# Experts' results finished in their tile of places and scattered to the output, instead of stored and gathered back

## The reference, cut to what matters

```python
xt = layernorm(x2)                         # 1250 x 512
probs = softmax(xt @ Ws + bs)              # 8 experts
prob_max, routes = max(probs), argmax(probs)
y = gelu(xt @ W1[e] + b1[e]) @ W2[e] + b2[e]     # for the token's e = routes
out = x2 + y * prob_max
```

## Time and profile before

| | |
|---|---|
| median of 3 runs | 1897.75 us (1884.08 to 1905.15) |
| the profiled execution | 1896.57 us, of which its span is 1894.8 us |
| busy: TensorE, VectorE, ScalarE, GpSimd | 83%, 68%, 47%, 58% |
| mean granted TensorE clock | 0.922 of full speed |
| from the first gather of the expert loop (1795.18 us) to the end of the span | 99.6 us |
| from the last bias add of the loop (ends 1871.46 us) to the end of the span | 23.3 us |

### The profile page before, as it was taken

The page is one execution under the profiler, slowest core; times in us unless marked ns, Lnnn a source line. Parts: engine busy times, 40 slices in busy tenths (PEclk is TensorE's granted clock), DMA queues, the critical chain, the costliest instruction groups (busy, mean ns, idle before and its releaser), DMA issues.

```text
span 1894.8 us, 20582 instructions
## 1 busy us (share of the span) xinstructions
PE 1570.2 (83%) x6464; PEld 672.8 (36%) x6464; DVE 1282.0 (68%) x2339; ACT 882.9 (47%) x977; POOL 1103.7 (58%) x1073
## 2 busy tenths in 40 slices
PE   2767877877798888987899988987999989888594
PEld 1223333332343333332433333333433333333573
DVE  6678876778246898777437867875458868765333
ACT  1454434445215556665316656664056666741120
POOL 4777777776016667776036777772067777740022
PEclk8898989888899999999899999998999999999597
DMA  6677666676147767776257787763388887755344
GB/s 221 199 200 200 178 194 186 181 233 203 48 116 225 204 199 211 208 208 181 64 164 229 229 245 225 227 196 106 96 245 231 236 247 221 210 147 191 113 131 154
DMA packets 119349, 355.34 MB, mean 188 GB/s; under 512 B 19760, under 2 KB 24200, under 8 KB 118981
## 3 DMA queue, kind: packets, MB, share of 16 engines
q0 software_dynamic: 83600, 274.01, 50.8%
q1 hardware_dynamic: 35637, 79.95, 13.1%
HBM read 333.93 MB, written 19.95 MB: 187 GB/s over the span
## 4 chain that ended last, share of the span: by engine, by line
PE 45%; POOL 16%; DVE 12%; DMA 10%; issue 8%; ACT 8%; DVEq 0%; SPq 0%; POOLq 0%; ACTq 0%
PE ps L1467 42%; POOL ring L683 14%; DVE ring L856 7%; ACT ring L1315 6%; DMA zT<-slot_table 6%; DMA ring<-x_table,idxT 3%; PE ps L1532 2%; DVE aggT L1166 1%; DVE xT L1066 1%; POOL ring L726 1%; DMA mix<-in_edge_weight 0%; ACT zT L1414 0%; DVE lg L900 0%; PE ps L1845 0%; POOL ring L735 0%
## 5 line engine op out<-in xcount | busy, mean ns | idle before, releaser
L683 POOL DMA_INDIRECT ring<-x_table,idxT x1018 | 1058.7, 1040 | 590.4 <-issue 294.7
L856 DVE SCALAR_TENSOR_TENSOR ring<-we_bc,wT,ring 128x512 f32<-128x512 f32 x1018 | 689.9, 746 | 126.5 <-DMA ring<-x_table,idxT 126.3
L1315 ACT ACTIVATE ring<-ring 128x3072 f32<-128x3072 f32 (+1 forms) x165 | 447.0, 2711 | 373.4 <-DVE ring L856 373.3
L1467 PE MATMUL ps<-ring,onehot 128*32 128x512 f32 x2036 | 371.1, 661 | 200.1 <-ACT ring L1315 194.1
L1467 PE MATMUL ps<-ring,zT 126*128 126x512 f32 x720 | 336.5, 597 | 0.0
L1358 ACT ACTIVATE ring<-ps 128x512 f32<-128x512 f32 x228 | 128.4, 600 | 230.0 <-PE ps L1467 229.9
L900 DVE TENSOR_REDUCE lg<-ps 128x128 f32<-128x512 f32 x208 | 143.0, 688 | 117.6 <-PE ps L1532 59.5
L1467 PE MATMUL ps<-ring 128*32 128x512 f32 (+2 forms) x672 | 215.1, 554 | 5.6 <-DVE aggT L1166 5.6
L1467 PEld LDWEIGHTS ps<-ring,onehot 128*32 128x32 f32 x2036 | 72.7, 113 | 409.4 <-ACT ring L1315 260.6
L1467 PEld LDWEIGHTS ps<-ring,zT 126*128 126x128 f32 x720 | 126.3, 190 | 132.4 <-issue 112.3
L1467 PE MATMUL ps<-w,zT 128*125 128x512 f32 (+2 forms) x320 | 148.6, 628 | 22.1 <-ACT zT L1414 22.1
(11 more groups left out here) (245 smaller groups left out, 1219.0 us busy)
## 6 DMA issues: line engine op xcount, KB each, us to landing
zT<-slot_table SPq DMA_DIRECT2D x36, 625.0 KB
ring<-x_table,idxT POOLq DMA_INDIRECT x1018, 3.8
w<-in_L_gnn_W SPq DMA_DIRECT2D x8, 1024.0 KB, 11.7
ring<-in_L_ffn_W SPq DMA_DIRECT2D x16, 512.0 KB, 9.7
x_table<-ring SPq DMA_DIRECT2D x30, 250.0 KB
x_table<-ring SPq DMA_DIRECT2D x17, 256.0 KB
y_table<-aggT SPq DMA_DIRECT2D x17, 256.0 KB, 2.0
ring<-in_x SPq DMA_DIRECT2D x1, 2304.0 KB
```

The costliest lines, as they stand in the source:

```text
L683: gp.indirect_dma_start(out=slots[:, k, u, :], out_offset=None, in_=table[:, :], in_offset=bass.IndirectOffsetOnAxis(ap=idx, axis=0)).then ...
L856: ins = v.scalar_tensor_tensor(out=slots[:, k, u, :], in0=we_bc[:, :], scalar=wT[:, c, u:u + 1], in1=slots[:, k, u, :], op0=ALU.mult, op1= ...
L1315: a.activation(at, at, ACT.Relu).then_inc(relu_done, 1)
L1467: return nc.tensor.matmul(o, lhsT, rhs, start=start, stop=stop)
```

## The change

SP now stores two tables' worth: x2 (from `mix`) into the second half of each row of a new DRAM table `pair_table` as soon as a tile of it is there, and the normalized rows into the first half. `y_table` and `slot_i` are gone. POOL's gather brings both halves, rows of 4 KB in place of 2 KB, into one of 6 buffers in place of 4; it waits for `y_out` of the tile six before, not for TensorE's transposes. The token numbers are counted from 1 (padding gives 0), so that the places without a token are known: `token_i` sends them to row 0, and `out_i` to an index of at least 7999, which the bounds check of the scatter leaves out. A second product of one-hots gives the chance of each place. After the second bias VectorE does one more instruction, chance times row plus residual, and POOL writes the finished rows to `out` by `out_i`, with an indirect DMA for each tile. The gathers and stores at the end are gone.

```diff
+        pair_table = nc.dram_tensor("pair_table", [N, 2, D], f32).ap()
...
-        xg = [aggflat[:, b * D:(b + 1) * D] for b in range(4)]
+        pairs = [aggflat[:, b * 2 * D:(b + 1) * 2 * D] for b in range(2)] + [zflat[:, KD * N - (b + 1) * 2 * D:KD * N - b * 2 * D] for b in range(3)]
+        pairs.append(xT[:, :, :].rearrange("p k n -> p (k n)")[:, NE * D:(NE + 2) * D])
+        xg = [ap[:, 0:D] for ap in pairs]
+        x2g = [ap[:, D:] for ap in pairs]
+        AHEAD = len(pairs)
...
             for t in range(NT):
+                sp.wait_ge(x2_ready, t + 1)
+                sp.dma_start(pair_table[t * P:t * P + rows(t), 1, :], mix[0:rows(t), t, :]).then_inc(rows_stored, 16)
+            for t in range(NT):
                 sp.wait_ge(staged, (L - 1) * NT + t + 1)
-                sp.dma_start(table[t * P:t * P + rows(t), :], ln_rows[t][0:rows(t), :]).then_inc(rows_stored, 16)
-
-            sp.wait_ge(x2_ready, NT)
+                sp.dma_start(pair_table[t * P:t * P + rows(t), 0, :], ln_rows[t][0:rows(t), :]).then_inc(rows_stored, 16)
+
             sp.dma_start(b2_bc, ...)
 
-            for j in range(NS):
-                sp.wait_ge(y_out, j + 1)
-                sp.dma_start(y_table[j * P:(j + 1) * P, :], yrow[j % 2]).then_inc(y_stored[j % 2], 16)
-            for t in range(NT):
-                sp.wait_ge(res_ready, t + 1)
-                sp.dma_start(out[t * P:t * P + rows(t), :], mix[0:rows(t), t, :]).then_inc(out_stored, 16)
-            sp.wait_ge(out_stored, NT * 16)
+            for b in range(2):
+                sp.wait_ge(out_stored[b], (NS + 1 - b) // 2 * 16)
...
             gp.wait_ge(token_ready, 1)
-            gp.wait_ge(rows_stored, NT * 16)
-            for j in range(NS):
-                if j >= 4:
-                    gp.wait_ge(xgT_done, j - 3)
-                gather_rows(xg[j % 4], table[:, :], token_i[:, j:j + 1], xg_got[j % 4])
-            for b in range(2):
-                gp.wait_ge(y_stored[b], (NS + 1 - b) // 2 * 16)
-            for t in range(NT):
-                gather_rows(ln_rows[t], y_table[:, :], slot_i[:, t:t + 1], yg_got[t])
+            gp.wait_ge(rows_stored, 2 * NT * 16)
+            BEHIND = 5
+            for i in range(NS + BEHIND):
+                if i < NS:
+                    if i >= AHEAD:
+                        gp.wait_ge(y_out, i - AHEAD + 1)
+                    gp.indirect_dma_start(out=pairs[i % AHEAD], out_offset=None, in_=pair_table.rearrange("n a d -> n (a d)"),
+                                          in_offset=bass.IndirectOffsetOnAxis(ap=token_i[:, i:i + 1], axis=0)).then_inc(xg_got[i % AHEAD], 16)
+                if i >= BEHIND:
+                    j = i - BEHIND
+                    if j == 0:
+                        gp.wait_ge(pads_out, 1)
+                    gp.wait_ge(y_out, j + 1)
+                    gp.indirect_dma_start(out=out, out_offset=bass.IndirectOffsetOnAxis(ap=out_i[:, j:j + 1], axis=0), in_=yrow[j % 2],
+                                          in_offset=None, bounds_check=N - 1, oob_is_err=False).then_inc(out_stored[j % 2], 16)
...
-            step(v.tensor_tensor(tile_oh, tile_oh, token[:, :].unsqueeze(2).to_broadcast([P, NT, NS]), ALU.mult))
+            step(v.tensor_tensor(token_oh, tile_oh, token[:, :].unsqueeze(2).to_broadcast([P, NT, NS]), ALU.mult))
             v.sem_inc(places_ready)
-            step(v.scalar_tensor_tensor(out=slot_i[:, :], in0=sc[:, 5, :], scalar=float(P), in1=sc[:, 4, :], op0=ALU.mult, op1=ALU.add))
+            step(v.tensor_tensor(sc[:, 7, :], sc[:, 3, :], valid[:, :], ALU.mult))
+            step(v.tensor_tensor(tile_oh, tile_oh, sc[:, 7, :].unsqueeze(2).to_broadcast([P, NT, NS]), ALU.mult))
+            v.sem_inc(chances_ready)
             v.wait_ge(token_done, 1)
-            step(v.tensor_copy(token_i[:, :], ps[2][:, 0:NS]))
+            step(v.tensor_scalar(token_i[:, :], ps[7][:, 0:NS], 1.0, 1.0, ALU.max, ALU.subtract))
             v.sem_inc(token_ready)
+            step(v.tensor_scalar(pad_of, ps[7][:, 0:NS], 0.0, BIG, ALU.is_equal, ALU.mult))
+            step(v.scalar_tensor_tensor(out=out_i, in0=ps[7][:, 0:NS], scalar=-1.0, in1=pad_of, op0=ALU.add, op1=ALU.add))
+            v.sem_inc(pads_out)
+            v.wait_ge(chances_done, 1)
+            step(v.tensor_copy(slot_chance, ps[6][:, 0:NS]))
...
                     if j >= 2:
-                        v.wait_ge(y_stored[j % 2], j // 2 * 16)
-                    v.tensor_tensor(yrow[j % 2], ps[6 + j % 2][:, :], b2_bc[...], ALU.add).then_inc(y_out, 1)
-            for t in range(NT):
-                r = rows(t)
-                v.wait_ge(yg_got[t], 16 + (16 * len(range(t, NS, 4)) if t < 4 else 0))
-                v.scalar_tensor_tensor(out=mix[0:r, t, :], in0=ln_rows[t][0:r, :], scalar=sc[0:r, 3, t:t + 1],
-                                       in1=mix[0:r, t, :], op0=ALU.mult, op1=ALU.add).then_inc(res_ready, 1)
+                        v.wait_ge(out_stored[j % 2], j // 2 * 16)
+                    step(v.tensor_tensor(yrow[j % 2], ps[6 + j % 2][:, :], b2_bc[...], ALU.add))
+                    v.scalar_tensor_tensor(out=yrow[j % 2], in0=yrow[j % 2], scalar=slot_chance[:, j:j + 1], in1=x2g[j % AHEAD], op0=ALU.mult, op1=ALU.add).then_inc(y_out, 1)
...
             for t in range(NT):
-                ins = mm(ps[2][:, 0:NS], place_oh[:, t, :], tile_oh[:, t, :], t == 0, t == NT - 1)
+                ins = mm(ps[7][:, 0:NS], place_oh[:, t, :], token_oh[:, t, :], t == 0, t == NT - 1)
             ins.then_inc(token_done, 1)
+            pe.wait_ge(chances_ready, 1)
+            for t in range(NT):
+                ins = mm(ps[6][:, 0:NS], place_oh[:, t, :], tile_oh[:, t, :], t == 0, t == NT - 1)
+            ins.then_inc(chances_done, 1)
```

28 lines of the change are left out of this document (14 added, 14 removed).

## The result

| | before | after |
|---|---|---|
| median of 20 runs each | 1898.42 us (1884.08 to 1905.84) | 1890.31 us (1877.93 to 1900.01) |
| ratio after / before, 95% interval | | 0.9958 (0.9941 to 0.9976) |
| the profiled execution, and its span | 1896.57, 1894.8 us | 1889.93, 1887.7 us |
| mean granted TensorE clock | 0.922 | 0.931 |

1880.7 us was forecast, 1868 to 1893 as the range. The time lies in the range, but the gain is 8 us where 17 were summed up.

What follows compares the result with a forecast made beforehand. The prediction took TensorE to bound the loop and the DMA engines the end. End -18.6, start +1.0 and last passes +0.5 gave -17.1 us, so 1880.7 us (-0.90%), range 1868 to 1893 us.

Steps and rivals of the forecast that it cites:

- The end: Behind the last second bias: 23.3 us of stores and gathers go, 4.7 us come, a gain of 18.6 us.
- The landing: Last scatter from issue to landing: 2.7 us taken, with 2.0 and 5.3 as the ends.
- The end behind a landing: From the last landing to the span's end: 0.9 us, read from the last store of `out`.
- The start: First gathers of the expert stage, 512 KB instead of 256: +1.0 us, ends 0 and +2.5.
- The loop: Expert tiles at a 4.10 us period: VectorE's, POOL's and DMA's added work costs nothing.
- The last passes: New VectorE instruction ahead of the last tile's copy and first bias: +0.5 us, ends 0 and 1.0.
- rival 4: In the loop VectorE waits for a scatter's landing before overwriting a `yrow`: 13 us, 1893 us; chance 0.04.
- The hidden second product: At the start, 20 more matmul instructions fall in TensorE's wait for the first gather: no cost, uncovered 4.45 us.
- rival 3: POOL bounds the loop if a scatter takes above 2.55 us; 1936 us at 6 us each; chance 0.06.
- x2's stores: SP's ten more stores between 1726 and 1753 us, at DMA share 0.15: covered; uncovered 8 us.
- Rival 2: At the start the added matmuls raise TensorE's clock early: 1.6 us saved, 1879 us; chance 0.07.
- Rival 1: The start costs more, as waits for 512 KB gathers delay the clock's rise: 5 us more, 1886 us; chance 0.11.

Runs made afterwards that it cites:

- e1: The changed kernel without the scatter of the 17th tile, which holds no token; end 6.44 us against 9.76, 90.72 us from `token_i` on against 93.27.
- e2: The kernel before with one late unused POOL instruction after the last residual sum, a gather or a memset; end 28.51 and 27.82 us against 24.03.
- e9: e8 with the first two tiles' normalized rows gathered alone (2 KB) and their residuals later; median 1879.12 us, ratio to the kernel before 0.9921.
- e12: The changed kernel with scatters without bounds check, each tile to its own table, experts' part missing from `out`; 89.52 us from `token_i` on against 93.27.
- e5: The changed kernel with places without a token gathering row p of the table in partition p, not all row 0; 91.86 us from `token_i` on against 93.27.
- e8: The changed kernel with the edits of e3, e5 and e7 together; median 1881.09 us, ratio to the kernel before 0.9929.
- e7: The changed kernel with four `yrow` buffers for finished rows in place of two; last passes 7.74 us against 8.87, 92.40 us from `token_i` on against 93.27.
- e3: The changed kernel with a tile's gather ahead of the scatter in POOL's queue; loop 53.34 us against 54.69, 90.16 us from `token_i` on against 93.27.
- e4: The changed kernel gathering only the normalized rows (2 KB), so residuals are wrong; start 17.16 us against 19.95, 89.14 us from `token_i` on against 93.27.
- after_again: The changed kernel once more, unaltered; median 1883.38 us, ratio to the kernel before 0.9953, 93.06 us from `token_i` on.
- e6: The changed kernel with unused 512-column matmuls before the places' product and before the first transposes; 93.81 us from `token_i` on against 93.27.

## Why the prediction was wrong, by its own steps

**The end, the failed step.** The forecast had 4.7 us behind the last second bias's end: 0.8 + 0.33 + 2.7 + 0.9. Measured are 9.07 = 9.76 - 0.69: 0.79 for L1306, 0.79 until the scatter starts, 7.49 from its start to the end of the span. The landing was not even underestimated: SP was through 2.1 us after the issue, below the 2.7. The step that failed is "The end behind a landing. The last store of `out` was issued at 1891.9 and the span ended 2.9 us later; less its 2.0 us of landing, 0.9 us". This took what follows a store by SP, with POOL idle for 5 us, for what follows an instruction of POOL. e1 and both e2 show in its place: the end comes 6.0 to 6.5 us behind the end of POOL's last instruction, of whatever kind (7.0 in e9). 7.49 - (2.7 + 0.9) = 3.9 us of the missing gain are here, 0.46 more are the scatter's late start, which is gone in e12 without the bounds check. The row that could have warned me was in the trace of before: POOL's drain at L223, which began while POOL still issued and ended 0.4 us ahead of SP's branch. An entry of 17.6 us under the last stores should have raised the question of what it waits for, and when it would end without them.

**The start, mis-sized: +1.0 said, +4.5 in the profiled pair, some +2.5 in the mean.** The mechanism was right and the size was not: the pair lies outside the bounds (0 to +2.5), the mean at their upper end. Its two halves: T1 was to move by 1.2 us, and moved by 2.7 (5.4 to 8.1 us after `token_i`; over all profiles with these gathers 7.7 to 8.3, against 5.4 to 6.2 in the three of the kernel before, in the mean 8.0 and 5.7, so 2.2 us). The 312 GB/s of the earlier trace rows, on which "the second lands some 1.7 us after the first" rested, come from gathers of rows that are all different; e5 shows that a gather of mostly one row is slower. With the equal rows spread (e5, e8) T1 is 1.1 us later than the kernel before's mean, about the 1.2 forecast; the other 1.2 us are the equal rows. The other half, from T1 to the first second bias, is the clock: 10.1, 11.6 and 11.1 us in the kernel before's three profiles, 10.4 to 12.0 in the six of the changed form. The profile of before that I read had drawn the shortest of all. The rise comes 3.4 to 6.8 us after the first transposes in the one form and 5.6 to 9.0 in the other. That it is the clock and nothing else, the table's 13 profiles with a T1 show: the rise comes 2.18 us (before) to 6.13 us (e7) after T1, and T1 to the first second bias takes 9.00 us plus 0.49 times that, within 0.01 us in each of them. On this the Trainium skill, page "TensorE: Matmul & The Clock Gate", Part 1, says that the number of cold matmuls varies from run to run of the same kernel; the rows agree, with the 1.5 us between equal kernels just named.

**The loop, a failed step worth 1.3 to 2.6 us.** "A gather goes out 1.6 us after the `y_out` of the tile six before, and TensorE wants it some 9 us later", so nothing. It goes out 2.3 us after that `y_out` (1815.86, the end of L1306) and TensorE wants it at 1822.28 (the transposes at 1814.07 and two periods), 4.1 us after the issue at 1818.15: I had counted a pass too many. The landing takes 4.30 us. For the gather of 4 KB rows the Trainium skill, page "DMA: Bandwidth & Descriptors", section "Anatomy of one DMA", would give by its fit 2.0 + 512 KB / 436 GB/s = 3.2 us, an estimate, by which TensorE would not have waited; the row says 4.3 and decides. e3 takes the loss away whole, and so do the smaller gathers of e4. Most of the spread from 1.3 to 2.6 us is one late landing towards the end of the loop, as in after_again, where a gather took 5.8 us and its period 5.55; why it is late, no run says.

**The last passes: +0.5 said, +1.55 measured.** 0.42 is the copy behind the new instruction, which is the forecast's mechanism (the row in e7); 1.13 is the `yrow` (e7), a wait that the forecast's term left out. That is rival 4's mechanism, priced there for the loop with 6.4 us between two uses. In the last passes second biases follow at 1.94 us, and the landing of 2.73 us does hold them.

**What held.** The hidden second product (e4's start). POOL's scatters, 0.985 to 1.033 us, so rival 3 never came near its 2.55. x2's stores: from POOL's last gather of the message layers to its first one of the expert stage it is idle for 107.6, 112.7 and 110.7 us in the three profiles of the kernel before, and for 106.6 to 113.3 in those of the changed form, the same in the mean, so nothing of the 8 us that the stores would cost uncovered is seen. Rival 2, a clock raised by the second product, did not come: the clock stayed at 0.50 through 40 matmuls of 17 columns (8.71 of 8.72 us busy), and in e6 it fell while they ran. Rival 1, a start 5 us dearer, is what the profiled pair nearly shows, half of it by chance.

Summed with the means: end -14.3, start +2.2 for T1 and +0.3 for the clock (11.2 against 10.9 us in the mean), loop +2.0 (the six profiles with 4 KB rows, its order of gather and scatter and the bounds check: 54.69 to 55.93, mean 55.34), last passes +1.55: -8.2 us, and the medians of 20 runs differ by 8.1. The agreement is closer than the means can promise: the end of the kernel before is one profile, its start three.

## What to carry to other kernels

Before a tail on one engine is taken away, look at the closing drain of each engine, not only at those that end the chain: here POOL's last instruction has to be over 6 us before the end. Leaving out POOL's last scatter won 3.3 us (e1: 6.44 for 9.76); giving the last work to another queue suggests itself and was not run. Where a transfer is made larger, look at the first one of a stage, with nothing ahead of it, and at the gap between what frees its buffer and who reads it, counted in passes on the row; what stands before it in the issuing queue belongs to that gap. And a start at half clock is a draw: read it from more than one profile before a microsecond of it is put down to a change.

## What the runs showed of the hardware

- POOL's closing drain ended 5.7 us (memset), 5.8 (gather), 6.2 to 6.4 us (scatters) after the end of POOL's last instruction, and 7.3 in the kernel before. No other engine's is as long: in the changed kernel TensorE's took 1.86 us, VectorE's 0.79, ScalarE's 0.45, SP's 7 ns.
- The second of six gathers in a row, 128 rows of 4 KB with over 100 of them equal, landed in 6.3 us, with the equal ones spread over the table in 5.05.
- A scatter with a bounds check starts 0.79 to 0.96 us after the end of what it waits for, without one (and to other tables) 0.28 us, while the row of the instruction stays at 0.97 to 1.03 us.
- TensorE's granted clock stayed at 1.00 through 2.49 us of idle time, fell to 0.50 some 1.5 us into matmuls of 17 columns that kept it busy without a gap, and rose 4.4 us into the wide ones behind them (e6).
- From the second tile's transposes on, each us that the rise of the clock came later cost 0.49 us, within 0.01 us over 13 profiles.
